# A sixteen-sublayer hybrid network on one core: router logits inside the norm, attention inputs prepared in another order, and one shared base product for the low-rank experts

## The reference

```python
# L0_ffn, used twice: top 2 of 8 experts, softmax gates
logits = xt @ Wr + br
...
h = relu(einsum('td,edh->teh', xt, W1) + b1)
out = einsum('ted,te->td', einsum('teh,ehd->ted', h, W2) + b2, gate)
...
# L3_ffn, used twice: the same with a 0/1 mask of the top 2 in place of the gates
probs = softmax(xt @ gate_w + gate_b); _, idx = top_k(probs, 2)
...
# three attentions with 16 heads of 8 channels (L0_attn_b causal and rotary, L2_attn_b plain,
# L3_attn_b with a spectral filter), and L3_attn_a with a local window of 64
scores = einsum('bhqd,bhkd->bhqk', q, k) / sqrt(dh)
out = einsum('bhqk,bhkd->bhqd', softmax(scores), v)
```

## Time and profile before

| what | value |
|---|---|
| median of 3 runs | 5376.97 us (5371.65 to 5380.79) |
| profiled execution, its own time | 5382.7 us |
| its span from first to last instruction | 5380.9 us |
| PE busy, share of the span | 4592.1 us, 85% |
| DVE busy | 3254.7 us, 60% |
| ACT busy | 2640.0 us, 49% |
| POOL busy | 1018.4 us, 19% |

### The profile page before, as it was taken

How to read it: one execution, slowest core, us unless ns; L and a number is a source line. 1 busy time by engine, 2 the same in 40 slices (tenths; PEclk the granted TensorE clock), 3 DMA queues, 4 the chain that set the end, 5 groups by cost and what they waited for, 6 DMA issues and landing times. The chain is left out here.

```text
span 5380.9 us, 65913 instructions
## 1 busy us (share of the span) xinstructions
PE 4592.1 (85%) x22439; PEld 1698.3 (32%) x22489; DVE 3254.7 (60%) x4647; ACT 2640.0 (49%) x4872; POOL 1018.4 (19%) x937
## 2 busy tenths in 40 slices
PE   6969999796079999767699997778978959999899
PEld 3422222342033333233122222355544412222244
DVE  4365555334865555153888883335983378888433
ACT  2325555334224444323488885334433338888733
POOL 0010000000027887800000000125960000000000
PEclk8979999898589999868799998878998969999989
DMA  1021000000000000000200000120000020000000
GB/s 60 20 61 37 32 28 23 13 20 0 0 8 3 5 3 5 22 10 0 66 25 25 27 24 2 36 64 16 1 1 20 13 59 25 26 30 27 3 20 20
DMA packets 44679, 118.25 MB, mean 22 GB/s; under 512 B 15154, under 2 KB 16178, under 8 KB 43346
## 3 DMA queue, kind: packets, MB, share of 16 engines
q1 hardware_dynamic: 37498, 97.49, 6.0%
q10 hardware_dynamic: 4320, 15.73, 0.8%
q0 software_dynamic: 2560, 1.19, 0.1%
HBM read 81.99 MB, written 19.01 MB: 19 GB/s over the span
## 5 line engine op out<-in xcount | busy, mean ns | idle before, releaser
L1074 DVE TENSOR_REDUCE 41_heads_mx<-41_heads_mps 128x1 f32<-128x1024 f32 x512 | 602.7, 1219 | 64.8 <-PE 41_heads_mps L952 63.7
L1074 DVE TENSOR_REDUCE 66_heads_mx<-66_heads_mps 128x1 f32<-128x1024 f32 x512 | 602.6, 1219 | 64.9 <-PE 66_heads_mps L952 63.8
L1048 ACT ACTIVATE 66_heads_p<-66_heads_sps 128x512 f32<-128x512 f32 x1024 | 552.8, 596 | 112.0 <-PE 66_heads_sps L973 108.2
L1048 ACT ACTIVATE 41_heads_p<-41_heads_sps 128x512 f32<-128x512 f32 x1024 | 552.7, 596 | 112.1 <-PE 41_heads_sps L973 108.1
L1074 DVE TENSOR_REDUCE 9_heads_mx<-9_heads_mps 128x1 f32<-128x1024 f32 (+7 forms) x384 | 333.0, 908 | 229.3 <-PE 9_heads_mps L955 223.5
L1931 ACT ACTIVATE 27_latent_heads_p<-27_latent_heads_ring 128x512 f32<-128x512 f32 x512 | 277.3, 595 | 385.5 <-PE 27_latent_heads_ring L1850 373.2
L1949 DVE TENSOR_REDUCE 27_latent_heads_mx<-27_latent_heads_ring 128x1 f32<-128x512 f32 x512 | 323.1, 684 | 197.5 <-PE 27_latent_heads_ring L1830 197.5
L1048 ACT ACTIVATE 9_heads_p<-9_heads_sps 128x512 f32<-128x512 f32 (+3 forms) x640 | 313.8, 532 | 232.0 <-PE 9_heads_sps L976 125.1
L973 PE MATMUL 41_heads_sps<-38_head_rows_qs,38_head_rows_ks 123*128 123x512 bf16 x1024 | 311.3, 386 | 4.9 <-ACT 41_heads_p L1048 4.9
L973 PE MATMUL 66_heads_sps<-61_head_rows_qs,61_head_rows_ks 123*128 123x512 bf16 x1024 | 310.8, 386 | 5.1 <-ACT 66_heads_p L1048 5.1
L1806 POOL TENSOR_TENSOR 27_latent_heads_psum<-27_latent_heads_psum,27_latent_heads_p 128x1024 f32<-128x1024 f32 x112 | 263.1, 2349 | 87.8 <-ACT 27_latent_heads_p L1931 87.8
(11 more groups left out here) (1103 smaller groups left out, 7301.2 us busy)
## 6 DMA issues: line engine op xcount, KB each, us to landing
4_experts_wbuf<-in_L0f_experts SPq DMA_DIRECT2D x8, 514.0 KB, 3.4
12_experts_wbuf<-in_L0f_experts SPq DMA_DIRECT2D x8, 514.0 KB, 3.3
60_experts_wbuf<-in_L3f_experts SPq DMA_DIRECT2D x8, 514.0 KB, 3.5
69_experts_wbuf<-in_L3f_experts SPq DMA_DIRECT2D x8, 514.0 KB, 3.5
46_hale_masks_qs<-scratch_q_parts SPq DMA_DIRECT2D x39, 96.0 KB
46_hale_masks_ks<-scratch_k_parts SPq DMA_DIRECT2D x39, 96.0 KB
5_head_rows_qs<-scratch_q_parts SPq DMA_DIRECT2D x28, 96.0 KB
5_head_rows_ks<-scratch_k_parts SPq DMA_DIRECT2D x28, 96.0 KB
```

Of the source, the lines that this page charges most:

```text
L1048: act.activation(pslot[x % PS][:, 0:CW - off], sps[e % SB][:, 0:CW - off], ACT.Exp, scale=SCALE / 2).then_inc(ex_done, 1)
L1074: dve.tensor_reduce(mx[h % 2][:, i, half:half + 1], mps[x % 2][:, 0:w], AX.X, ALU.max).then_inc(mx_taken, 1)
```

## The change

First, `residual_and_norm` takes a router. PE makes the logits chunk by chunk inside the norm: chunk 0 between the transposes of chunks 1 and 2, chunks 1 to 3 behind the last transposes; DVE adds the bias as its last instruction there, into a lasting tile `g.logits`. `route` has no logit products any more and starts with the picks.

Second, in `route` ACT copies `gateT_f` and DVE copies `gateT`, where DVE did both (in the gates and mask modes).

Third, `prepare_heads` goes by parts over both halves instead of by halves. DVE takes over POOL's subtractions and its fill of ones, ACT takes over the copies of V, the bias of V becomes a product with one row of ones on PE, the fills of the key buffers become small DMAs on SP, and the key rows of head 0 are issued by POOL while SP issues the query rows.

Fourth, `lora_experts` makes `wi` times `nT` once per unit. It adds the first expert's correction, ACT reads the bank, then PE adds into the same bank the difference of the second and the first expert's correction (the constant `pair` gets a negative copy for that), and ACT reads it again. The inputs of chunk c + 1 are made inside the units of chunk c, and only chunk 0's stand ahead.

```diff
@@ residual_and_norm
+                def score_chunk(c):
+                    wait_for_chunk(c)
+                    if c == 0:
+                        pe.wait_ge(router[2], 16)
+                        pe.wait_ge(x_ready, 2)
+                    for i in range(c * TPC, (c + 1) * TPC):
+                        ins = pe.matmul(head[0][:, i * E_N:(i + 1) * E_N], nT[:, tile(i)], router[0], start=True, stop=True)
+                    ins.then_inc(logits_ready, 1)
...
+                    if c == 1 and router is not None:
+                        score_chunk(0)
...
+                for c in range(1, NC if router is not None else 0):
+                    score_chunk(c)
...
+                        dve.wait_ge(logits_ready, NC)
+                        dve.tensor_tensor(g.logits[:].rearrange("p t e -> p (t e)"), head[0][:, 0:NT * E_N], router[1], ALU.add).then_inc(logits_done, 1)
@@ route
+                for c in range(NC if need_f else 0):
+                    act.wait_ge(turned_ready, c + 1)
+                    act.activation(g.gateT_f[:, chunk(c)], turned_f[c % 2][:], ACT.Identity).then_inc(f_copied, 1)
...
-                dve.wait_ge(logits_ready, 1)
-                ch.link(dve.tensor_tensor(v[:], logit_ps[:], br.rearrange("p (t e) -> p t e", e=E_N), ALU.add))
...
-                    if need_f:
-                        ch.link(dve.tensor_copy(g.gateT_f[:, chunk(c)], turned_f[c % 2][:]))
@@ HeadRows
+        for k in self.ks:
+            eng.dma_start(k[self.fill_at:self.fill_at + 3, :].rearrange("p (n k) -> p n k", k=FILL),
+                          self.fill.unsqueeze(1).to_broadcast([3, T // FILL, FILL])).then_inc(self.filled, 16)
@@ prepare_heads
+                    ins = pe.matmul(vps[i // TPC][:, tile(i % TPC)], nT[:, tile(i)], Wv, start=True, stop=bv is None)
+                    if bv is not None:
+                        ins = pe.matmul(vps[i // TPC][:, tile(i % TPC)], g.W["ones_row"], bv[0:1, :], start=False, stop=True)
...
+                for s in "qk":
+                    dve.tensor_copy(half(parts[s][0], 0), half(whole[s], 0)).then_inc(part[s][0][0], 1)
                 for i in range(2):
+                    for s in "qk":
+                        dve.wait_ge(part[s][0][i], 1)
+                        dve.tensor_tensor(half(rest[s], i), half(whole[s], i), half(parts[s][0], i), ALU.subtract).then_inc(less[s][0][i], 1)
+                for i in range(2):
+                    for s in "qk":
+                        dve.wait_ge(part[s][1][i], 1)
+                        dve.tensor_tensor(half(rest[s], i), half(rest[s], i), half(parts[s][1], i), ALU.subtract).then_inc(less[s][1][i], 1)
+                dve.memset(Vt[:, :, :, DH:ROW], 1.0)
+                for n, t in enumerate(twice):
+                    wait_for_part(dve, "q", n + 1)
+                    dve.tensor_scalar(t[:], parts["q"][n + 1][:], 2.0, None, ALU.mult).then_inc(two_done, 1)
...
+                for s in "qk":
+                    act.activation(half(parts[s][0], 1), half(whole[s], 1), ACT.Identity).then_inc(part[s][0][1], 1)
+                for a in (1, 2):
+                    for i in range(2):
+                        for s in "qk":
+                            act.wait_ge(less[s][a - 1][i], 1)
+                            act.activation(half(parts[s][a], i), half(rest[s], i), ACT.Identity).then_inc(part[s][a][i], 1)
+                act.wait_ge(v_ready, 1)
+                for c in range(NC):
+                    act.activation(Vt[:, c * TPC:(c + 1) * TPC, :, 0:DH], vps[c][:].rearrange("p (t h d) -> p t h d", t=TPC, d=DH),
+                                   ACT.Identity).then_inc(v_done, 1)
...
+                for a in range(3):
+                    wait_for_part(pool, "k", a)
+                    rows.copy_keys(pool, 0, a, rows.first_keys_in)
...
+                rows.fill_keys(sp)
+                for a in range(3):
+                    wait_for_part(sp, "q", a)
                     rows.copy_queries(sp, 0, a, rows.rows_in[0])
@@ lora_experts
+                pe.wait_ge(ready, 16)
+                enter(0)
+                for u in range(UNITS):
+                    c, f = divmod(u, NF)
+                    base(u)
+                    if u == 0:
+                        enter_change(0)
+                    first(u)
+                    if u >= 1:
+                        change(u - 1)
+                    if u >= 2:
+                        output(u - 2)
+                    if c + 1 < NC and f == 0:
+                        enter(c + 1)
+                    if c + 1 < NC and f == 2:
+                        enter_change(c + 1)
+                change(UNITS - 1)
+                output(UNITS - 2)
+                output(UNITS - 1)
```

More of the change, by code:

```diff
@@ L1531, in _ @@
                     pe.matmul(vps[:], g.pair_sum[:], g.gateT[:, chunk(c)], start=True, stop=True).then_inc(v_ready, 1)
[L1532 to L1538 removed]
+                    if c:
+                        pe.wait_ge(am_ready, 2 * c)
@@ L1564, in _, with relu @@
[L1564 to L1568 removed]
+                def relu(u, which, there, done):
+                    act.wait_ge(there, u + 1)
+                    if u >= 2:
+                        act.wait_ge(hs_ready, u - 1)
+                    f = u % NF
+                    act.activation(hr[which][u % 2][:], hps[u % BANKS][:], ACT.Relu, bias=W["L2f_bi"][:, f:f + 1]).then_inc(done, 1)
```

262 lines of the change are left out of this document (122 added, 140 removed).

## The result

The changed kernel takes 5302.74 us (median of four runs, 5301.03 to 5311.85); the kernel before took 5377.97 beside it. The ratio is 0.9865, 95% interval 0.9848 to 0.9882: 75 us less, where the forecast was 92. Its profiled execution took 5303.91 us, its span is 5302.1, and the mean granted clock is 0.912 (0.910 before). Spans compared with spans, 78.8 us went.

A forecast was written before the change was run, and what follows sets the result against it. No engine was taken to bound the whole; stages stand one behind the other. Gains of 11.4 + 2.0 + 41 + 37.7 = 92 us gave 5290.6 from the profiled 5382.7, forecast 5285 from the median, range 5268 to 5314.

The forecast's parts named there:

- Logits and gates: Six norms and routers: logits made inside the norm gain 11.4 us; gate copies on two engines, four times, gain 2.0.
- the table load: Router start: ACT's 1.28 us exponential table load loses its cover, costing 0.6 us four times in pair and mask modes.
- Low-rank experts: Two PE-bound expert stages: one of five products per unit removed, inputs moved between units; 20.4 us each, 41 in all.
- Rival B: Expert units: new hand-overs do not fit, PE waits for ACT, 13.7 us lost twice; 5312 us, chance 0.09.
- Preparations: Four head preparations: next block starts at 15.2 us instead of 25.7; gain 10.5 three times, 6.2 in local attention, 37.7 total.
- DVE's and ACT's chain: Preparations: subtractions, casts, then V copies end at 15.1 us, or 13.8 with queuing; 14.5 taken as the block's end.
- POOL's price: Preparations: each of POOL's 12 key DMA issues costs 0.555 us, the last two from 12.3 to 13.4.
- A: Preparations: POOL's key issues wait until DVE's subtractions are over, 13 us later in all; 5298 us, chance 0.13.
- C: Preparations: a key issue on POOL costs several us, making the kernel slower, 5415 us at 4 us each; chance 0.03.
- D: Preparations: each key issue held for two DVE subtractions, 3.0 us, leaving 6 us of gain; 5371 us, chance 0.04.
- which has nothing else there: Preparations: V's bias products add 32 records on PE, which was said to have nothing else there; no time priced.
- 12 query DMAs at 0.65: Preparations: SP issues head 0's twelve query copies at 0.65 us each, done at 12.5 us, before ACT ends.

The follow-up runs named there:

- e2: Changed kernel with head 0's key copies issued by SP again, in turns with the query copies, instead of by POOL; 5310.91 us.
- e4: Changed kernel with V's bias as one 512-column product per PSUM bank, ahead of V's products, instead of sixteen narrow alternating ones; 5295.92 us.
- g2: On top of `e4`, the constant rows of the key tiles issued by POOL instead of SP; 5297.99 us.

## Why the prediction was right, and where not

**Logits and gates, 13.4 forecast.** Right step by step: 14.2 in the trace, 15.9 by itself with an interval of about 7 to either side. Chunk 0's logits cost nothing, the 24 records behind the tail took 5.12 (5.2 forecast), the table load came out from under its cover.

**Low-rank experts, 41 forecast.** Right, 43.1 in the trace, 66.6 and 66.2 us a stage against 66.9; the second gained more because it had been longer before (88.6 against 87.3). Rival B fell: PE had 0.6 us of idle time in the window of 57 us above.

**Preparations, 37.7 forecast, 13.2 found at the loops' starts.** DVE's and ACT's chain was nearly right, 13.5 us (13.8 to 15.1 forecast), and so was POOL's price, 0.518 against 0.555, so that A, C and D fell. The Trainium skill ("SBUF — State Buffer", The "DVE blocks DMA" trap) speaks of DVE's two-port modes; what ran beside POOL's issues here were subtractions with two float32 inputs in SBUF, and the trace shows no wait. Two steps failed.

The first is the sentence that the bias products of V go on PE, "which has nothing else there". PE had nothing else to do, but ACT's copy of V waits for them. The step asked who stands in PE's way and not who waits for PE, and gave no price to the 32 records. At V's own price in the rotary stage before (5.54 us for 32 records, 0.173 each, mostly at the half clock) 64 records would have made 11 us, ahead of ACT's 12.3, and would still have looked free. They took 23.2 (rotary) and 21 (plain), because each alternation of one-row and 128-row weights costs, and because PE was at the half clock: 0.50 in the whole of the rotary stretch, and 0.50 from 2528 on in the plain one (0.89 in the 4 us before). Size: 10.8 us.

The second is "12 query DMAs at 0.65". The number was read off a queue that issued 32 KB every 0.66 us, that is at 49 GB/s, and was taken for the price of an issue. It was that, but the transfers were hardly faster. The trace before had the rate in a window of the filtered block, where SP's queue is nearly the only one that moves anything (the last two columns are the DMA share and the GB/s). A window in which issuing alone can set the rate doesn't show a limit of the transfers. What the prediction took without a reason is that two queues would carry about twice these 46 GB/s:

```profile
4347.00:4362.00 15.00, 0.00 (x0) 0.00 (x0) 8.06 (x10) 5.61 (x6) 6.75 (x4) 0.50 0.33 46
```

Two queues halve the issuing; they hardly carry more: 49 GB/s with both. The Trainium skill has both halves of it, and the prediction weighed neither. "DMA: Bandwidth & Descriptors", Issuing engines are not separate DMA queues, says that several issuing engines save only the sequencers' time, which `e2` bears out. "SBUF — State Buffer", Door 1: The DMA port swizzle, says, from transfers between HBM and SBUF, that a transfer's rate goes by how many of 16 ports its partitions reach, 27.2 GB/s each; 8 rows in a row reach two, 16 four and 24 six, an estimate from that page of 54, 109 and 163 GB/s. Measured were 49 to 57, 127 and 142. The order and the first size agree; the 16-row copies ran above the page's figure and the 24-row ones below, so there the measurement stands. By the same estimate the 24 copies of a block take 14.5 us from the first one on, and the block 17 us or more.

The size of the second: 3.9 us in the filtered block (19.2 to 15.3 with half the bytes, 15.6 with wide copies), 1.8 in the local one, and, since `e4`'s other two blocks end at the same 19.2 to 19.5 us, 3.9 each there, which no run shows by itself. 13.2 + 10.8 + (3 x 3.9 + 1.8) = 37.5, the forecast 37.7. So with both limits gone the sum of the prediction would come out, as far as these runs show; 7.8 of the 37.5 are carried over from the filtered block, and the end of the block has other parts than the forecast gave it.

**The total.** 92.1 forecast, less 24.5 in the preparations, plus 0.8 and 2.1 where routers and experts did a little better, 7.3 for the local loop and 1.0 elsewhere: 78.8, the span's difference. Without the local loop's 7.3 the forecast would have missed by more, so a part of its nearness was luck.

## What to carry to other kernels

Price a step by who waits for its result, also when its engine is idle; and when a queue's issues are being split over two queues, divide bytes by time first: if the rate is one that copies of so few rows don't exceed anywhere, the second queue gives nothing. Copies between SBUF tiles want more rows each rather than more queues. Keep one-row bias products together, one wide one for each bank ahead of the products that accumulate on it, rather than one behind each.

## What the runs showed of the hardware

- Float32 products that alternate between weights of 128 rows and of one row took 0.36 us a record at the half clock (23.2 us for 64) and 0.22 at nearly the full one (16 records in 3.48 us at 0.89); V alone took 0.21 and 0.12. In groups of eight records of a kind it was 0.25 at the half clock.
- Copies from SBUF to SBUF of 8 partitions x 4096 B ran at 46 GB/s over one queue, with a DMA share of 0.33, and at 49 over two, with a share of 0.48; 16 partitions at 127 GB/s and a share of 0.87; 24 at 142 and 0.70.
- SP stalls in issuing once transfers lag: single issues of 1.2 to 2.65 us (3.99 in `g2`) where 0.624 is its own price; POOL's issues beside it, and beside DVE's subtractions with two inputs in SBUF, stayed at 0.518 (0.585 at most).
- From the issue of a 32 KB store to DRAM to the issue of the reads that waited for it passed 3.2 to 5.3 us.
